# One tap of the depthwise convolution moved from VectorE to ScalarE and GpSimd, between the rows of a GpSimd chain

## What is computed

```
zxbcdt = u @ in_proj_w                       # 256 -> 1288 columns: z | x,B,C | dt
dt   = softplus(zxbcdt[..., -8:] + dt_bias)  # the step sizes, one per head
conv = sum(xp[:, i:i+L, :] * cw[i] for i in range(4)) + conv_bias   # 4 taps back in time
xBC  = conv * sigmoid(conv)                  # silu, 768 channels
y    = ssd(x * dt, A * dt, B, C) + D * x     # decays exp(A dt) over the sequence
y    = rmsnorm(y * silu(z)) @ out_proj_w
```

## Time and profile before

| what | us |
|---|---|
| median of 3 runs | 1392.12 (1389.46 to 1392.37) |
| the profiled execution | 1387.37 |
| its span from first to last instruction | 1385.5 |
| TensorE busy in the span | 1252.3 (90%) |
| VectorE busy | 941.3 (68%) |
| ScalarE busy | 677.8 (49%) |
| GpSimd busy | 271.7 (20%) |

### The profile page before, as it was taken

One profiled execution on the slowest core, in us unless ns is written; L12 is line 12 of the kernel. 1 busy time (PEld: TensorE's weight loads), 2 busy tenths in 40 slices (PEclk: granted clock), 3 DMA queues, 4 the chain that ended last, 5 costly groups with the idle time before them and its releaser, 6 DMA issues. The chain is left out here.

```text
span 1385.5 us, 25269 instructions
## 1 busy us (share of the span) xinstructions
PE 1252.3 (90%) x8404; PEld 1108.9 (80%) x8404; DVE 941.3 (68%) x2935; ACT 677.8 (49%) x1527; POOL 271.7 (20%) x281
## 2 busy tenths in 40 slices
PE   5889998999899898998998989899897479999997
PEld 4668988867799797778988967799797458888886
DVE  6867767777576676756767776577676875555553
ACT  4737627653565474635636654466374413333332
POOL 2001005110000330100005110000250084333332
PEclk9999999999999999999999999999999579999999
DMA  6026400010452001016500010453611012222221
GB/s 250 1 47 144 115 17 1 1 61 1 116 138 53 16 1 62 1 29 152 126 16 1 1 61 1 106 125 75 229 61 34 1 23 39 38 35 38 39 40 23
DMA packets 45661, 80.38 MB, mean 58 GB/s; under 512 B 8448, under 2 KB 18176, under 8 KB 45024
## 3 DMA queue, kind: packets, MB, share of 16 engines
q1 hardware_dynamic: 37376, 69.19, 18.5%
q0 software_dynamic: 6720, 9.18, 4.1%
q10 hardware_dynamic: 1440, 0.39, 0.1%
HBM read 28.01 MB, written 8.78 MB: 27 GB/s over the span
## 5 line engine op out<-in xcount | busy, mean ns | idle before, releaser
L1036 ACT ACTIVATE b_pp<-b_pp,b_nm 128x256 f32<-128x256 f32 x256 | 116.0, 501 | 83.6 <-DVE b_nm L1074 82.7
L912 PEld LDWEIGHTS bank<-b_va,b_pt 128*128 128x128 f32 x1024 | 128.6, 193 | 4.4
L912 PE MATMUL bank<-b_va,b_pt 128*128 128x65 f32 x1024 | 129.2, 270 | 0.0
L1371 PE MATMUL bank<-c_v,c_pt 128*128 128x68 f32 x768 | 102.2, 269 | 4.1 <-DVE c_pt L1597 3.5
L1371 PEld LDWEIGHTS bank<-c_v,c_pt 128*128 128x128 f32 x768 | 97.2, 191 | 7.8 <-DVE c_pt L1597 7.0
L1074 DVE CUSTOM_DVE_ANT_0 b_pp<-bank,mask 128x256 f32<-128x256 f32 x256 | 97.0, 417 | 0.0
L100 PE MATMUL bank<-e_up_low,e_xh 128*128 x210 | 90.8, 432 | 6.6 <-DVE e_xl L208 5.0
L1899 ACT ACTIVATE e_th<-bank 128x512 f32<-128x512 f32 x35 | 21.0, 601 | 152.8 <-PE bank L102 152.8
L1349 PE MATMUL bank<-c_kv,c_qv 128*128 128x128 f32 (+1 forms) x512 | 89.2, 298 | 0.0
L197 PE MATMUL bank<-identr 128*128 128x512 f32 x274 | 75.6, 426 | 14.9 <-DVE a_cv L617 8.2
L1589 DVE CUSTOM_DVE_ANT_0 c_pp<-bank,const 128x128 f32<-128x128 f32 (+1 forms) x256 | 80.0, 350 | 11.3 <-PE bank L1349 10.8
(11 more groups left out here) (403 smaller groups left out, 3658.2 us busy)
## 6 DMA issues: line engine op xcount, KB each, us to landing
b_kst<-b_kh SPq DMA_DIRECT2D x128, 128.0 KB, 2.3
k_low_twice<-b_kl SPq DMA_DIRECT2D x128, 128.0 KB, 2.4
b_qst<-b_ql SPq DMA_DIRECT2D x64, 128.0 KB, 2.4
raw_up<-in_w SPq DMA_DIRECT2D x4, 768.0 KB, 10.4
raw_down<-in_w SPq DMA_DIRECT2D x4, 768.0 KB, 12.1
XN<-in_x SPq DMA_DIRECT2D x5, 512.0 KB, 3.8
context<-in_ctxT SPq DMA_DIRECT2D x4, 512.0 KB, 5.9
mask<-in_mask SPq DMA_DIRECT2D x4, 512.0 KB, 6.8
```

The source lines that it names most:

```text
L912: ins = pe.matmul(O2[u % 2][:, at:at + VW], pt[:, n % 2, kt * S + qt * P:kt * S + (qt + 1) * P], va[:, b * QT + kt, 2 * j + hp, :], start= ...
L1036: act.activation(pp[:, n % 3, qt, :], pp[:, n % 3, qt, :], ACT.Exp, bias=nm[:, n % 4, qt:qt + 1], scale=-1.0).then_inc(s["probs_exp"], 1)
L1371: ins = pe.matmul(OB[u % 2][:, at:at + AKV * AVW], pt[:, n % 4, i * P:(i + 1) * P], v[:, b * QT + kt].rearrange("p a b -> p (a b)"), start ...
```

## The change

The oldest of the four taps (k = 3, which reads the bank shifted by three tokens) leaves VectorE. ScalarE evicts the tile a second time, scaled by that tap, into `y[:, n % 2]` (semaphore `tap_scaled`). GpSimd adds it to `cv`, 2 x 253 elements per partition, once VectorE's two remaining taps are done (`add_tap`, semaphore `tap_added`). GpSimd's six additions are spread over its queue: tiles 0 and 1 ahead of the step size chain, 2, 3 and 4 inside it, and 5 behind its last row.

VectorE's `convolve` now starts after ScalarE's second eviction (`tap_scaled` in place of `conv_begun`). ScalarE's tanh and VectorE's silu wait for `tap_added` in place of `conv_done`; ScalarE's second eviction of tile n waits for the addition of tile n - 2, whose buffer it takes. TensorE waits for `tap_scaled` as well before it overwrites a bank; the warming matmuls still wait for `conv_done` of the last tile.

```diff
--- before.py
+++ after.py
@@ -377,17 +377,29 @@
                         ins = pool.tensor_scalar(K["dd"][:, k, c], K["const"][:, C_ID + j * HD:C_ID + (j + 1) * HD],
                                                  K["dpar"][:, h:h + 1], None, ALU.mult)
                 ins.then_inc(w["diagonal_set"], 1)
+            def add_tap(n):
+                pool.wait_ge(s["tap_scaled"], n + 1)
+                pool.wait_ge(s["conv_done"], n + 1)
+                out = cv[:, n % 3, :].rearrange("p (b l) -> p b l", b=2)[:, :, TAPS - 1:]
+                tap = y[:, n % 2, :].rearrange("p (b l) -> p b l", b=2)[:, :, 0:S - TAPS + 1]
+                pool.tensor_tensor(out, out, tap, ALU.add).then_inc(s["tap_added"], 1)
+
+            add_tap(0)
+            add_tap(1)
             pool.wait_ge(s["den_inverted"], 1)
             ch.link(pool.tensor_tensor(zz[:], e[:], den[:], ALU.mult))
             ch.link(pool.tensor_tensor(z2[:], zz[:], zz[:], ALU.mult))
             ch.link(pool.tensor_scalar(acc[:], z2[:], 1.0 / 15, None, ALU.mult))
             for m in (13, 11, 9, 7, 5, 3):
+                if m in (11, 7, 3):
+                    add_tap(2 + (11, 7, 3).index(m))
                 ch.link(pool.tensor_scalar(acc[:], acc[:], 1.0 / m, None, ALU.add))
                 ch.link(pool.tensor_tensor(acc[:], acc[:], z2[:], ALU.mult))
             ch.link(pool.tensor_scalar(acc[:], acc[:], 1.0, 2.0, ALU.add, ALU.mult))
             ch.link(pool.tensor_tensor(acc[:], acc[:], zz[:], ALU.mult))
             ch.link(pool.tensor_tensor(dt[:], acc[:], r[:], ALU.add))
             pool.tensor_tensor(a[:], dt[:], K["A"][:].unsqueeze(1).to_broadcast([P, GT, NH]), ALU.mult).then_inc(s["decay_rates"], 1)
+            add_tap(CT - 1)
             pool.wait_ge(s["context_high"], 1)
             pool.tensor_tensor(context_low[:], CX[0][:].rearrange("p k n -> p (k n)"), context_high[:].bitcast(F32),
                                ALU.subtract).then_inc(s["context_low"], 1)
@@ -410,6 +422,7 @@
             for n in range(CT):
                 if n >= 2:
                     pe.wait_ge(s["conv_done"], n - 1)
+                    pe.wait_ge(s["tap_scaled"], n - 1)
                 w0 = DI + ORDER[n] * P
                 for k in range(KD):
                     ins = split_matmul(pe, J[n % 2][:], [w[:, k, w0:w0 + P] for w in W["win"]],
@@ -536,14 +549,17 @@
                         act.wait_ge(s["conv_silu"], n - 2)
                     act.activation(cv[:, n % 3, :], J[n % 2][:], ACT.Identity, bias=K["tapb"][:, f:f + 1],
                                    scale=K["taps"][:, f, TAPS - 1:TAPS]).then_inc(s["conv_begun"], 1)
+                    if n >= 2:
+                        act.wait_ge(s["tap_added"], n - 1)
+                    act.activation(y[:, n % 2, :], J[n % 2][:], ACT.Copy, scale=K["taps"][:, f, 0:1]).then_inc(s["tap_scaled"], 1)
                 if g and n == CT:
                     act.wait_ge(s["logits_ready"], 1)
                     act.activation(K["logits"][:, (g - 1) * GT:g * GT, :], T[0][:, 0:GT * NE].rearrange("p (t e) -> p t e", e=NE),
                                    ACT.Copy).then_inc(s["logits_copied"], 1)
                 if n >= 1:
-                    act.wait_ge(s["conv_done"], n)
-                    if n == CT:
-                        act.wait_ge(s["conv_silu"], CT - 2)
+                    act.wait_ge(s["tap_added"], n)
+                    if n >= 3:
+                        act.wait_ge(s["conv_silu"], n - 2)
                     act.activation(th[:, (n - 1) % 2, :], cv[:, (n - 1) % 3, :], ACT.Tanh).then_inc(s["conv_tanh"], 1)
                 if n == 1:
                     act.wait_ge(s["minus_abs_dt"], 1)
@@ -608,22 +624,22 @@
 
             def convolve(n):
                 f = ORDER[n]
-                dve.wait_ge(s["conv_begun"], n + 1)
+                dve.wait_ge(s["tap_scaled"], n + 1)
                 out = cv[:, n % 3, :].rearrange("p (b l) -> p b l", b=2)
                 src = J[n % 2][:].rearrange("p (b l) -> p b l", b=2)
-                for k in range(1, TAPS):
+                for k in range(1, TAPS - 1):
                     if k > 1:
                         ch.sync()
                     ins = dve.scalar_tensor_tensor(out=out[:, :, k:], in0=src[:, :, 0:S - k],
                                                    scalar=K["taps"][:, f, TAPS - 1 - k:TAPS - k], in1=out[:, :, k:],
                                                    op0=ALU.mult, op1=ALU.add)
-                    if k < TAPS - 1:
+                    if k < TAPS - 2:
                         ch.then(ins)
                 ins.then_inc(s["conv_done"], 1)
 
             def activate(n):
                 dve.wait_ge(s["conv_tanh"], n + 1)
-                dve.wait_ge(s["conv_done"], n + 1)
+                dve.wait_ge(s["tap_added"], n + 1)
                 dve.scalar_tensor_tensor(out=xs[:, ORDER[n], :], in0=th[:, n % 2, :], scalar=1.0, in1=cv[:, n % 3, :],
                                          op0=ALU.add, op1=ALU.mult).then_inc(s["conv_silu"], 1)
...

```

More of the change, by code:

```diff
@@ L2052, in _ @@
             ch.sync()
-SEM_A = ("context_high context_low v_projected next_ctx next_mask x_times_dt decay_rates decay_sums decays_masked dt_projected dt_copied dt_turned "
+SEM_A = ("tap_scaled tap_added context_high context_low v_projected next_ctx next_mask x_times_dt decay_rates decay_sums decays_masked dt_projected dt_copied dt_turned "
          "conv_done conv_projected z_projected conv_silu x_turned small_bank_read chunk_scores "
```

## The result

The changed kernel took 1392.05 us (median of 12 runs, 1391.3 to 1395.32), the kernel before 1389.71 us (12 runs beside it): a ratio of 1.0021 with a 95% interval of 1.0011 to 1.003. It is slower, as forecast, with an interval that lies above 1, by 2.3 us where +9.1 was forecast. In a second session on one chip it was 1392.04 against 1389.0, ratio 1.0026 [1.0014, 1.0038].

A forecast was written before the change was run, and what follows sets the result against it. TensorE's path through the warming matmuls to L463 was taken to bound the stage; GpSimd's chain would replace it. 3 x 2.04 + 3.02 = +9.1 us on 1392.1 gave 1401.2 us, range 1391 to 1407.

The forecast's parts named there:

- the mechanism named: Convolution stage: GpSimd's chain with six additions and port waits, then tanh, activation and gates, delays L463 by 2.04 us (group 2).
- The rival without collisions: Convolution stage: short VectorE SBUF steps slip in beside GpSimd's additions; -4.6 us, 1387.5 us; faster got chance 0.10.
- four collisions of 0.36: GpSimd's polynomial: steps wait for the activations of four tiles, 0.36 us each; 0.75 us more than today a group.
- addition 1.28: GpSimd: each addition of 506 elements takes 1.28 us, from subtraction rows; four in the chain add 5.12 us.
- the prediction's own slope: GpSimd's chain of six additions: 0.1 us on one addition changes a group by some 0.56 us.
- the 2.04 of three groups: Decay sums of L463 in groups 0, 2 and 3: start 2.04 us later in each.
- the 3.02 of group 1: Decay sums of L463 in group 1, which has 0.98 us less to hide things in: 3.02 us later.
- The draw rival: GpSimd's addition takes near 1.0 us; 0.4 in three groups, 1.4 in group 1: +2.6, 1394.7 us; chance 0.11.
- The lower bound of 0.71: GpSimd's addition at its cheapest, 0.71 us, from a one-input cast of 1024; would give -3, 1389 us.
- +1.20: GpSimd's polynomial in group 2 starts 1.20 us later, behind additions 0 and 1 and blocked VectorE steps.
- The sum's last step: TensorE from L463 on: a later L463 moves all that follows by as much, so +9.1 us in total.
- The much slower case: Additions of 1.55 us, or TensorE's clock staying down behind L463, some 2 us a group; 1407 to 1409; chance 0.09.

The follow-up runs named there:

- gates_first: Changed kernel with VectorE's four gates of z issued ahead of the last tile's activation instead of behind it; 1392.83 us, ratio 1.0026 to the kernel before.
- short_add: Changed kernel with GpSimd's additions cut from 2 x 253 to 2 x 125 elements; 1381.95 us, ratio 0.9946 to the kernel before.
- layout_price: Changed kernel with the additions of tiles 2, 3 and 4 given other shapes and operand starts, changing what they compute; 1394.82 us, timed once.
- add_beside: Kernel before, all taps kept on VectorE, plus five additions a group of idle data on GpSimd; 1397.5 us, ratio 1.0058.
- before_filled: Kernel before with twelve more warming matmuls in each cross attention, filling two idle gaps of TensorE; 1384.59 us, ratio 0.9958.
- after_filled: Changed kernel with twelve more warming matmuls in each cross attention, filling two idle gaps of TensorE; 1392.22 us, ratio 1.0014 to the kernel before.

## Why the prediction came out as it did

**Slower, by the mechanism named: right.** The polynomial, with the additions in it, reaches the end of the stage, and the gated z behind the last tanh sets L476 (0.85 us of idle time, ended by `a_zg`). gates_first and short_add moved L476 by moving just these two things. The rival without collisions falls: `a_e` and `a_den` waited, and four steps of the chain took 0.55, 0.74, 0.49 and 0.76. That is some 1.5 us above the 0.25 to 0.29 of such steps, close to the four collisions of 0.36 that were forecast.

**The term "addition 1.28" was mis-sized: 1.08.** By the prediction's own slope, 0.56 us a group for 0.1 us, the 2.04 of three groups becomes 2.04 - 2 x 0.56 = 0.92 and the 3.02 of group 1 becomes 1.90, in sum +4.7; the three profiles show +4.6 to +5.6, and by group 1.96 in group 1 and 1.16 and 0.99 in groups 2 and 3. I took the nearest row by size and operation; what differed was where the operands start, which layout_price showed. With three of the six additions at the long price its stages cost some 3 us more than the changed kernel's. The +8.3 of add_beside, though near +9.1, is no test of the sum: nothing waits for its additions, VectorE keeps its taps, the last of which ends 2.2 us later, and in three groups L474 idles for ScalarE's masks, which hang on the decay rates.

The draw rival named the cheaper addition with 0.11, for another reason than the one found: the fixed part is there, and the time per element is less. That the median's +2.3 lies near that rival's +2.6 is luck, since the stages lost twice as much. It is luck too that 1392.05 lies within 1391 to 1407: the forecast counted from a median of 3 runs, 1392.12, which 12 runs put at 1389.71. The lower bound of 0.71 for an addition is not what the earlier trace rows give: with a fixed part of 0.2 the cast of 1024 scales to 0.62.

The Trainium skill (GPSIMD Engine Reference, "Elementwise — side-by-side cycle accounting") had 2.6 cycles per element, from which the prediction estimated 1.10 us. The change's own additions come near it in total, at 1.08, but as a fixed part of 0.2 us and 1.75 ns per element, where 2.6 cycles at 1.2 GHz make an estimate of 2.17; the same 506 elements with operands that start alike take 1.26 and 1.27.

**"+1.20" at the polynomial's start was +0.66.** Some 0.40 of the 0.54 is the price of the two additions again. The rest is that `a_r` slipped in at 554.45, 0.02 us before addition 0, in every group.

**The sum's last step failed: that L463 moves all that follows by as much.** The stages lost 4.6 to 5.6 us and the median 2.3 to 3.0. What the step left out are the falls of the granted clock, which cost each kernel a different amount. In the cross attention, behind TensorE's two idle gaps, a fall costs mostly 1.4 us a group. With the gaps filled the difference is 7.6, so they had hidden some 4 us of it (0.42% less 0.12%, uncertain by some 0.23%). The higher granted clock of the changed kernel, 0.966 against 0.964, fits this. Where the kernel before lost more stays open. In the cross attention its two profiles lie 2.2 and 4.7 us above before_filled's, the changed kernel's three 2.0 to 2.9 above after_filled's, and two or three of four groups are slow in either, which doesn't make 4 us. One candidate, which no run separates, is its convolution stage, which takes 1.0 us more in a group when the warming runs wholly at 0.50; the changed kernel's stage hides that. Open as well are the 1.7 us by which 7.6 exceeds the stages: the two intervals leave some 2.7 us uncertain, and other parts of a single execution, such as the experts (309.0 to 311.5 us), vary by as much in any kernel.

**The much slower case,** in which the granted clock stays down behind the wait, did not come: it was 1.00 in the 14.3 us from L476 on.

## What to carry to other kernels

A price taken from the nearest row holds for that row's operands: before a chain of small instructions is hung on it, look for a row whose operands start as the new ones will, or widen the range by the spread. Work given to an engine that seems idle is paid where its in-order chain meets the end of the stage, so give it only as much as its slack: with two tiles of six the stages lost nothing, with six they lost 5 us. And where stages say one thing and the median another, compare the stages behind between two profiles of one kernel: here two idle gaps of TensorE and the clock behind them blurred the differences, and filling them brought the medians into the order of the stages.

## What the runs showed of the hardware that was not expected

- GpSimd's two-input addition of 506 elements takes 1.08 us with the output and the first input starting three elements further in than the second input, and 1.26 with all three starting alike.
- TensorE's granted clock, after idle gaps of 1.68 and 1.81 us, fell to 0.50 in one execution, and after 1.71 and 1.81 us, with the same busy time around them, stayed at 1.00 in another of the same code. In the four profiles with twelve matmuls that compute nothing in each cross attention it did not fall there, and these made the kernel before faster, ratio 0.9958 [0.9942, 0.9974].
